# Graph stage of a two-layer graph and expert network: both matrix products as sums of half-precision products, degrees taken earlier

## The chip, the cores and the metric

The kernel runs on one core of a Trainium2 chip. What is timed is the device time in microseconds of one execution. Executions of the kernel before took 1640.42, 1648.84 and 1653.16 us; the median is 1648.84 us.

## The reference, cut to what matters

625 nodes with 768 features go through four steps, each added to its input: a normalized-adjacency graph layer, an attention and expert layer, a graph attention layer and a second expert layer. The change lies in the first of them:

```
edge_index = jnp.stack([src, dst])                 # 20625 edges, one loop per node among them
x = x + _L0_gnn_ref(_layernorm(x), edge_index, L0_gnn_W, L0_gnn_b)

def _L0_gnn_ref(x, edge_index, W, b):              # (cut)
    row, col = edge_index with one more loop per node
    deg  = segment_sum(ones, col)                  # how many edges end in a node
    dinv = rsqrt(deg)
    h    = x @ W                                   # 625x768 by 768x768
    msg  = h[row] * (dinv[row] * dinv[col])[:, None]
    return segment_sum(msg, col) + b
```

The kernel writes this with a matrix C of edge counts (625 x 625): out = dinv * ((C + I)^T (dinv * (z W))) + b, where z is the normalized x. C's zeros also give the two masks of the later graph attention layer.

## The kernel before, in words

Nodes are held as NT = 5 tiles of P = 125 rows, features as KC = 6 chunks of 128. Every engine has its own instruction stream, written out by hand in order; semaphores order the engines among each other, and a wait holds all that is behind it on its engine. There is no planner. PSUM has 8 banks of 512 float32 columns.

**Counts.** SyncE's queue starts the input transfers and then, from `raw01`, the writes of zeros to `x_slots` and `y_slots` (L825 to L831). For each of 165 chunks of 125 edges VectorE builds two one-hot blocks (`one_hot`, L1370 and L1371) and TensorE multiplies them (`edge_chunk`, L1992 and L1995). Chunks fall into six groups. After a group ScalarE and VectorE part the packed sums (`upper_counts`, `lower_counts`) and VectorE adds them to `CT` (`upper_added` L1391, `lower_added` L1401). Group 5 is the last. VectorE norms the rows into `z` on the way.

**First product.** TensorE transposes z in 30 pieces (L1976); VectorE and ScalarE copy them out of PSUM by turns (L1325, L1017). Then TensorE makes z W in float32, for each tile six chunks by 512 and by 256 columns (L2019), and ScalarE copies each tile to `xf` (L1045).

**Masks and degrees.** TensorE transposes C (L2029). VectorE makes the bfloat16 mask out of it (L1449) and sums the degrees (L1451), takes their root (`root_of`, L1303 to L1307) and scales xf (L1459). GpSimd meanwhile makes a float32 mask `absent` of CT (L936) and adds it to the logarithm of CT (L1042, L938).

**Second product.** For each tile i, TensorE makes C^T xf in float32, five tiles by 512 and by 256 columns (L2038); VectorE adds the own row (L1494), scales and adds to `xres` (L1496), takes mean and variance, norms the row into `z` (L1485) and splits its heads with ScalarE (L1055, L1057, L1488), all in `heads_normed`. Bank pairs alternate, so product i waits until VectorE has read product i - 2.

**The fence** after it (`fence(..., F_GRAPH)`) lets an engine go on once PE, VectorE, ScalarE and GpSimd have all come there. The attention of the next stage starts with TensorE's L2054.

Of the kernel before, what the change touches and what calls it, by code (L numbers as in the profile page):

```python
# [82 lines left out]
def bass_gnn_moe_stack(nc, x, src, dst, gnn_w, vecs, gate0, gate1, units0, units_s, units1,  # L83
                       bias_out, w_heads, attn_lr, out):
    ctx = ExitStack()
    with ctx:
# [1203 lines left out]
        def _(dve):  # L1290
# [30 lines left out]
            def transposed_out():  # L1321

                for c in range(0, KC, 2):
                    dve.wait_ge(s_tp, KC * (count["tp"] // 3) + c + 1)
                    nc.vector.tensor_copy(tD[:, c, :].rearrange("p (t n) -> p t n", t=NT),  # L1325
# [1092 lines left out]
```

## Time and profile before

| What | Value |
|---|---|
| Executions | 1640.42, 1648.84, 1653.16 us |
| Profiled execution, its own time | 1650.27 us |
| Its span | 1648.7 us |
| Mean granted clock of TensorE | 0.95 |
| PE busy | 1492.9 us, 91% |
| VectorE busy | 1276.5 us, 77% |
| ScalarE busy | 858.5 us, 52% |
| GpSimd busy | 331.3 us, 20% |

The profile is of one execution. PE is TensorE's matrix products, PEld its loads of the stationary operand, DVE is VectorE, ACT ScalarE, POOL GpSimd. Busy shares are means over the whole span; a stage is to be read by itself. A granted clock of 1.00 is 2.4 GHz, one of 0.50 is 1.2 GHz. A line number is that of the instruction in the kernel.

### The profile page before, as it was taken

How to read it: one execution, taken by the hardware profiler on the slowest of the kernel's cores; microseconds unless marked ns; L12 is line 12 of the kernel's file. 1: busy time of each engine (PE TensorE's matmuls, PEld its weight loads, DVE VectorE, ACT ScalarE, POOL GpSimd, SP SyncE). 2: the span in 40 equal slices, each digit the busy share in tenths (PEclk: the TensorE clock that was granted, in tenths of full speed). 3: DMA queues.
4: the chain of work that ended last, by engine and by line, in shares of the span. 5: the costliest groups of instructions: out<-in, count | busy, mean ns of one | idle time of the engine just before them, and what ended most of it. 6: DMA issues, size and time to landing. Idle time of an engine off the chain costs nothing.

```text
span 1648.7 us, 36612 instructions
## 1 busy us (share of the span) xinstructions
PE 1492.9 (91%) x14493; PEld 1271.4 (77%) x14493; DVE 1276.5 (77%) x2195; ACT 858.5 (52%) x1220; POOL 331.3 (20%) x254
## 2 busy tenths in 40 slices
PE   7987887887799999999999779966999999999996
PEld 5664545665567899999999554436899999999995
DVE  8998376775556678888888778967888878888785
ACT  1112116775544567776765234554666666666661
POOL 0004003665030000000003036755420000000050
PEclk9998898999799999999999887986999999999999
DMA  7640000000465688898886110123988888888883
GB/s 203 157 112 0 0 1 10 1 1 5 169 190 179 229 276 290 289 315 297 299 296 210 52 30 26 32 94 96 336 290 288 294 298 300 284 300 287 296 281 104
DMA packets 55554, 297.59 MB, mean 180 GB/s; under 512 B 14063, under 2 KB 14319, under 8 KB 32433
## 3 DMA queue, kind: packets, MB, share of 16 engines
q1 hardware_dynamic: 41761, 263.23, 47.0%
q0 software_dynamic: 13712, 33.26, 7.3%
q8 instruction: 53, 0.87, 0.2%
q14 instruction: 28, 0.23, 0.0%
HBM read 264.07 MB, written 32.34 MB: 180 GB/s over the span
## 4 chain that ended last, share of the span: by engine, by line
PE 58%; DVE 7%; DMA 3%; POOL 3%; ACT 2%; issue 2%; SPq 0%; DVEq 0%; ACTq 0%; POOLq 0%
PE ps L727 13%; PE ps L706 9%; PE ps L708 9%; PE ps L710 9%; PE ps L2190 5%; PE ps L2173 5%; PE ps L2302 3%; POOL wl L980 2%; DMA ext<-in_units 2%; DVE wl L583 1%; PE ps L739 1%; PE ps L690 1%; DVE big L1842 1%; DMA xf<-y_slots,slots_i 1%; PE ps L2137 1%
## 5 line engine op out<-in xcount | busy, mean ns | idle before, releaser
L706 PE MATMUL ps<-big,wh 128*128 128x176 f16 x2160 | 495.3, 239 | 8.5 <-DVE wl L583 6.6
L710 PE MATMUL ps<-big,wl 128*128 128x176 f16 x2160 | 495.4, 238 | 0.0
L708 PE MATMUL ps<-big,wh 128*128 128x176 f16 x2160 | 495.4, 238 | 0.0
L727 PE MATMUL ps<-big,wh 128*128 128x176 f16 x2160 | 262.8, 238 | 3.1 <-DVE big L617 3.1
L727 PE MATMUL ps<-big,wl 128*128 128x176 f16 x1080 | 248.9, 239 | 0.0
L583 DVE SCALAR_TENSOR_TENSOR wl<-ext,wh 128x2304 f16<-128x2304 f32 x90 | 229.6, 2551 | 0.9 <-issue 0.6
L583 DVE SCALAR_TENSOR_TENSOR wl<-raw,wh 128x2304 f16<-128x2304 f32 x90 | 229.4, 2549 | 0.0
L502 ACT ACTIVATE wh<-raw 128x2304 f16<-128x2304 f32 x90 | 190.4, 2117 | 58.2 <-PE ps L727 53.7
L706 PEld LDWEIGHTS ps<-big,wh 128*128 128x128 f16 x2160 | 208.3, 96 | 12.5 <-DVE wl L583 6.8
L502 ACT ACTIVATE wh<-ext 128x2304 f16<-128x2304 f32 x90 | 190.5, 2117 | 50.0 <-PE ps L727 34.5
L708 PEld LDWEIGHTS ps<-big,wh 128*128 128x128 f16 x2160 | 210.8, 98 | 0.2
L710 PEld LDWEIGHTS ps<-big,wl 128*128 128x128 f16 x2160 | 207.8, 96 | 0.0
L727 PEld LDWEIGHTS ps<-big,wh 128*128 128x128 f16 x2160 | 188.2, 97 | 4.7 <-DVE big L617 4.0
L1992 PE MATMUL ps<-wl 126*128 126x314 f16 x660 | 113.7, 300 | 20.9 <-DVE wl L1371 20.9
L945 POOL TENSOR_TENSOR ext<-raw,ext 125x625 f16<-125x625 f32 x60 | 80.3, 1339 | 150.4 <-ACT ext L1086 149.8
L727 PEld LDWEIGHTS ps<-big,wl 128*128 128x128 f16 x1080 | 104.4, 97 | 0.0
L980 POOL TENSOR_TENSOR wl<-wl,logs 125x625 f32<-125x625 f32 x60 | 83.2, 1413 | 67.8 <-DVE wl L1870 67.8
L469 POOL DMA_DIRECT2D y_slots<-big x16 | 11.7, 733 | 419.7 <-ACT big L532 419.7
L2302 PE MATMUL ps<-raw,wh 125*65 125x512 f32 x240 | 86.2, 507 | 6.2 <-ACT raw L1216 6.2
L1992 PEld LDWEIGHTS ps<-wl 126*128 126x128 f16 x660 | 59.6, 99 | 37.2 <-DVE wl L1371 16.4
L613 DVE TENSOR_TENSOR big<-ps,ext 128x176 f32<-128x176 f32 x108 | 36.5, 338 | 66.6 <-ACT ext L525 66.5
L463 POOL DMA_DIRECT2D big<-x_slots x17 | 12.7, 745 | 343.6 <-PE ps L690 305.1
(352 smaller groups left out, 2819.6 us busy)
## 6 DMA issues: line engine op xcount, KB each, us to landing
raw<-in_units SPq DMA_DIRECT2D x54, 1152.0 KB, 5.5
ext<-in_units SPq DMA_DIRECT2D x54, 1152.0 KB, 6.4
raw<-in_units SPq DMA_DIRECT2D x36, 1153.0 KB, 6.0
ext<-in_units SPq DMA_DIRECT2D x36, 1153.0 KB, 7.1
raw<-in_units_s SPq DMA_DIRECT2D x16, 769.0 KB, 4.5
ext<-in_units_s SPq DMA_DIRECT2D x16, 769.0 KB, 4.4
x_slots<-raw SPq DMA_DIRECT2D x1, 8976.0 KB
big<-x_slots POOLq DMA_DIRECT2D x17, 528.0 KB, 8.7
```

The costliest lines, as they stand in the source:

```text
L502: nc.scalar.activation(wh[:, u % RING, 0:ph.wide], raw[u % RING][:, 0:ph.wide], ACT.Copy, scale=WS).then_inc(ph.hi, 1)
L583: nc.vector.scalar_tensor_tensor(out=wl[:, u % RING, 0:ph.wide], in0=raw[u % RING][:, 0:ph.wide], scalar=WS, in1=wh[:, u % RING, 0:ph.wide ...
L706: nc.tensor.matmul(o, wh[:, u % RING, w_], x_, start=c == 0 and m == 0, stop=False, skip_group_check=True)
L708: nc.tensor.matmul(o, wh[:, u % RING, w_], xTl[:, c, 0:ph.n], start=False, stop=False, skip_group_check=True)
L710: ins = nc.tensor.matmul(o, wl[:, u % RING, w_], x_, start=False, stop=c == KC - 1, skip_group_check=True)
L727: ins = nc.tensor.matmul(o, l_[:, u % RING, w_], r_, start=first and k == 0 and c % 2 == 0, stop=last and k == 2, skip_group_check=True)
L945: nc.gpsimd.tensor_tensor(pT[:, 1, h % 2, :, own], key_blocks(n), pT[:, 0, h % 2, :, own], ALU.subtract).then_inc(s_wlo, 1)
L980: nc.gpsimd.tensor_tensor(power[:, (h * NT + t) % 4, :], power[:, (h * NT + t) % 4, :], logs[:, t, :], ALU.add).then_inc(s_masked, 1)
L1992: nc.tensor.matmul(ps[:, at + i * BANK:at + i * BANK + TH], hot[0:k, s, i * P:i * P + 128], hot[0:k, s, TP:TP + TH], start=first, stop=las ...
L2173: ins = nc.tensor.matmul(shared_up(j)[:, 0:n], l_[:, j % RING, w_], r_[:, c, t0 * P:t1 * P], start=c == 0 and k == 0, stop=c == KC - 1 and ...
L2190: ins = nc.tensor.matmul(shared_sum(t)[:, n0:n1], l_[:, j % 2, own], r_[:, j % RING, D + n0:D + n1], start=fresh and k == 0, stop=last and ...
L2302: ins = nc.tensor.matmul(sumsT[:, n0:n1], values[:, t, h, :], prob[:, t, n0:n1], start=t == 0, stop=t == NT - 1)
```

## The change

- **First product.** z is transposed as before, but the first three chunks already between the count products of group 5, the other three after it. ScalarE writes the float16 high parts (`xsh`, `rows_high`), VectorE the rests (`xsl`, `rows_low`). W is scaled by 64 and split too: `wgh` on ScalarE, `wgl` on VectorE, ahead of the last additions to CT. z W becomes three float16 products: high by high, rest by high, high by rest (`node_products`).
- **Degrees.** After tiles 0 and 1 of the first product, TensorE multiplies CT by a column of ones (25 products of one column). VectorE takes the root from them.
- **Rows scaled.** dinv is applied while z W leaves PSUM: `node_high` (ScalarE, float16 `hth`) and `node_low` (VectorE, rest `htl`). The scaling pass L1459 goes.
- **Counts split.** `CTh` (ScalarE) and `CTl` (VectorE) are the float16 high part and rest of CT. The second product is CTh by hth, CTh by htl, CTl by hth; the own row comes in by an identity, so the addition L1494 goes.
- **Masks.** The turns of CT go one by one behind the tiles of the first product (`counts_turned`); VectorE's loop is now: `node_low(t)`, `masked_counts(t)`, then the addition of the bias row to `xres` (before: in one go at L1443).
- **GpSimd.** `absent` lies in `z` and waits for `node_low(0)`.
- **Normed rows.** z of a tile is written by ScalarE (scale and bias from VectorE, one small operation more there), not by VectorE's L1485.

The diff, cut: lines that are only names and constants, and longer removed blocks, are left out.

```diff
...
-absent = wl[0:P, :, :].rearrange("p a n -> p (a n)").bitcast(F32)[:, 0:NT * T]\
-    .rearrange("p (t n) -> p t n", t=NT)
+absent = z[:, :, :].rearrange("p t d -> p (t d)")[:, 0:NT * T].rearrange("p (t n) -> p t n", t=NT)
+CTh = wl[0:P, :, :].rearrange("p a n -> p (a n)")[:, 2400:2400 + NT * T].rearrange("p (t n) -> p t n", t=NT)
+CTl = wl[0:P, :, :].rearrange("p a n -> p (a n)")[:, 5600:5600 + NT * T].rearrange("p (t n) -> p t n", t=NT)
+wgh = raw01[:, 0, 0:KC * D // 2].bitcast(F16).rearrange("p (c n) -> p c n", c=KC)
...
+def z0_turned(c):
+    at = (4 * BANK) + c % 3 * NT * 128
+    return ps[:, at:at + NT * 128].rearrange("p (t n) -> p t n", t=NT)[:, :, 0:P]
+def node_sum(t):
+    return bank(t % 3 * 2, 2)[0:P, 0:D]
...
-    pool.wait_ge(s_unp, 3 * len(GROUPS))
+    pool.wait_ge(s_nl, NL_H + 1)
     nc.gpsimd.tensor_scalar(absent, CT, 0.0, NEG, ALU.is_equal, ALU.mult).then_inc(s_logs, 1)
     pool.wait_ge(s_logs, 2)
     nc.gpsimd.tensor_tensor(logs[:, :, :], logs[:, :, :], absent, ALU.add).then_inc(s_logs, 1)
...
+    def rows_high(half):
+        act.wait_ge(s_tp, 3 * half + 3)
+        for c in range(3 * half, 3 * half + 3):
+            nc.scalar.activation(xsh[:, c, :].rearrange("p (t n) -> p t n", t=NT), z0_turned(c), ACT.Copy)\
+                .then_inc(s_nh, 1)
+    def node_high(t):
+        act.wait_ge(s_hmm, t + 1)
+        nc.scalar.activation(hth[:, t, :], node_sum(t), ACT.Copy, scale=rs[:, 3, t:t + 1]).then_inc(s_nh, 1)
...
-    for g in range(1, len(GROUPS)):
+    for g in range(1, len(GROUPS) - 1):
         upper_counts(g)
-    transposed_out()
+    act.wait_ge(s_zero, 48)
+    act.wait_ge(s_wg, 16)
+    for c in range(KC):
+        nc.scalar.activation(wgh[:, c, :], wg[:, c, :], ACT.Copy, scale=WS).then_inc(s_nh, 1)
+    rows_high(0)
+    upper_counts(len(GROUPS) - 1)
+    rows_high(1)
     act.wait_ge(s_unp, 3 * len(GROUPS))
+    nc.scalar.activation(CTh, CT, ACT.Copy).then_inc(s_nh, 1)
+    root()
+    count["sq"] += 1
+    act.wait_ge(s_var, count["sq"])
+    node_high(0)
+    node_high(1)
     nc.scalar.activation(logs[:, :, :], CT, ACT.Ln, bias=least[:, 0:1]).then_inc(s_logs, 1)
-    for t in range(NT):
-        act.wait_ge(s_hmm, t + 1)
-        nc.scalar.activation(xf[:, t, :], ps[0:P, (t % 2) * 1024:(t % 2) * 1024 + D], ACT.Copy)\
-            .then_inc(s_hev, 1)
-    root()
+    for t in range(2, NT):
+        node_high(t)
     act.wait_ge(s_logs, 3)
     for t in range(NT):
         count["sq"] += 1
...
+        nc.scalar.activation(z[:, t, :], xres[:, t, :], ACT.Identity, bias=pair[:, 2, t, 0:1],
+                             scale=pair[:, 3, t, 0:1])
     fence(act, F_GRAPH)
-    act.wait_ge(s_zero, 48)
...
+    def rows_low(half):
+        dve.wait_ge(s_nh, NH_Z + 3 * half + 3)
+        for c in range(3 * half, 3 * half + 3):
+            nc.vector.tensor_tensor(xsl[:, c, :].rearrange("p (t n) -> p t n", t=NT), z0_turned(c),
+                                    xsh[:, c, :].rearrange("p (t n) -> p t n", t=NT),
+                                    ALU.subtract).then_inc(s_nl, 1)
...
     g = len(GROUPS) - 1
+    rows_low(0)
     lower_counts(g)
+    rows_low(1)
+    for c in range(KC):
+        dve.wait_ge(s_nh, NH_W + c + 1)
+        nc.vector.scalar_tensor_tensor(out=wgl[:, c, :], in0=wg[:, c, :], scalar=WS, in1=wgh[:, c, :],
+                                       op0=ALU.mult, op1=ALU.subtract).then_inc(s_nl, 1)
     upper_added(g)
     lower_added(g)
-    transposed_out()
-    dve.wait_ge(s_vec[0], 16)
...
     step(nc.vector.tensor_scalar(upto[:, :, :], upto[:, :, :], 0.0, None, ALU.is_ge))
     gates_split(0)
+    dve.wait_ge(s_deg, 1)
+    nc.vector.tensor_scalar(rs[:, 0, :], bank(6)[0:P, 0:NT], 1.0, None, ALU.add).then_inc(s_var, 1)
+    dve.wait_ge(s_nh, NH_CT + 1)
+    nc.vector.tensor_tensor(CTl, CT, CTh, ALU.subtract).then_inc(s_nl, 1)
+    root_of(dinv[:, :])
+    step(nc.vector.tensor_scalar(rs[:, 3, :], dinv[:, :], 1.0 / WS, None, ALU.mult))
+    nc.vector.memset(dot[0:1, 0:1], 0.0).then_inc(s_var, 1)
+    def node_low(t):
+        dve.wait_ge(s_nh, NH_H + t + 1)
+        nc.vector.scalar_tensor_tensor(out=htl[:, t, :], in0=node_sum(t), scalar=rs[:, 3, t:t + 1],
+                                       in1=hth[:, t, :], op0=ALU.mult, op1=ALU.subtract).then_inc(s_nl, 1)
+    def masked_counts(i):
+        dve.wait_ge(s_cT, i + 1)
+        nc.vector.tensor_scalar(mask[:, i, :].rearrange("p (k n) -> p k n", k=NT), tiles5(bank(6, 2), P), 0.0,
+                                NEG, ALU.is_equal, ALU.mult).then_inc(s_cdv, 1)
+    dve.wait_ge(s_vec[0], 16)
+    dve.wait_ge(s_vec[1], 16)
     for t in range(NT):
...
+        node_low(t)
+        masked_counts(t)
+        nc.vector.tensor_tensor(xres[:, t, :], xres[:, t, :], vec[:, 0, :], ALU.add)
...
+        step(nc.vector.scalar_tensor_tensor(out=tmp[:, 0:1], in0=mv[:, t, 0:1], scalar=-1.0, in1=inv[:, 0:1],
+                                            op0=ALU.mult, op1=ALU.mult))
         nc.vector.memset(dot[0:1, 0:1], 0.0).then_inc(s_var, 1)
-        nc.vector.tensor_scalar(z[:, t, :], xres[:, t, :], mv[:, t, 0:1], inv[:, 0:1],
-                                ALU.subtract, ALU.mult)
...
     for i in range(NT):
         dve.wait_ge(s_agg, i + 1)
-        step(nc.vector.tensor_tensor(z[:, i, :], ps[0:P, (i % 2) * 1024:(i % 2) * 1024 + D], xf[:, i, :],
-                                     ALU.add))
-        nc.vector.scalar_tensor_tensor(out=xres[:, i, :], in0=z[:, i, :], scalar=dinv[:, i:i + 1],
+        nc.vector.scalar_tensor_tensor(out=xres[:, i, :], in0=bank(i % 2 * 2, 2)[0:P, 0:D], scalar=dinv[:, i:i + 1],
                                        in1=xres[:, i, :], op0=ALU.mult, op1=ALU.add).then_inc(s_aggv, 1)
         dve.wait_ge(s_aggv, i + 1)
         heads_normed(i)
...
+    def rows_transposed_0(half):
+        for c in range(3 * half, 3 * half + 3):
             for t in range(NT):
-                ins = nc.tensor.transpose(o[:, t * 128:t * 128 + P], rows_[:, t, c * 128:(c + 1) * 128],
-                                          ident[0:P, 0:P])
+                ins = nc.tensor.transpose(z0_turned(c)[:, t, :], z[:, t, c * 128:(c + 1) * 128], ident[0:P, 0:P])
             ins.then_inc(s_tp, 1)
-            count["tp"] += 1
-    def transposed(k):
-        pe.wait_ge(s_tpe, 3 * k)
-        pe.wait_ge(s_tpa, 3 * k)
     def edge_chunk(c, g, first, last):
...
             pe.wait_ge(s_unp, 3 * g - 5)
         for c in range(j0 * EU, j1 * EU):
             edge_chunk(c, g, c == j0 * EU, c == j1 * EU - 1)
-    pe.wait_ge(s_rowsok, R_Z0)
-    pe.wait_ge(s_unp, 3 * len(GROUPS) - 5)
-    transpose_rows(z)
-    transposed(1)
-    pe.wait_ge(s_wg, 16)
+            if g == len(GROUPS) - 1 and c == (j0 + 3) * EU - 1:
+                pe.wait_ge(s_rowsok, 1)
+                pe.wait_ge(s_unp, 3 * len(GROUPS) - 5)
+                rows_transposed_0(0)
+    def node_products(t, n0, n1):
+        for k, (l_, r_) in enumerate(((xsh, wgh), (xsl, wgh), (xsh, wgl))):
+            if t == 0 and n0 == 0 and k == 0:
+                pe.wait_ge(s_nh, NH_Z + KC)
+                pe.wait_ge(s_nh, NH_W + KC)
+            if t == 0 and n0 == 0 and k == 1:
+                pe.wait_ge(s_nl, NL_Z + KC)
+            for c in range(KC):
+                if t == 0 and n0 == 0 and k == 2:
+                    pe.wait_ge(s_nl, NL_W + c + 1)
+                ins = nc.tensor.matmul(node_sum(t)[:, n0:n1], l_[:, c, t * P:(t + 1) * P], r_[:, c, n0:n1],
+                                       start=k == 0 and c == 0, stop=k == 2 and c == KC - 1)
+        if n1 == D:
+            ins.then_inc(s_hmm, 1)
+    def counts_turned(i):
+        if i:
+            pe.wait_ge(s_cdv, i)
+        for k in range(NT):
+            ins = nc.tensor.transpose(bank(6, 2)[0:P, k * 128:k * 128 + P], CT[:, k, i * P:(i + 1) * P],
+                                      ident[0:P, 0:P])
+        ins.then_inc(s_cT, 1)
+    pe.wait_ge(s_nl, NL_Z + 3)
+    rows_transposed_0(1)
     pe.wait_ge(s_unp, 3 * len(GROUPS) - 2)
...
+    for t in range(2):
+        node_products(t, 0, BANK)
+        node_products(t, BANK, D)
     pe.wait_ge(s_unp, 3 * len(GROUPS))
     for i in range(NT):
-        if i >= 2:
-            pe.wait_ge(s_cdv, i - 1)
-        o = bank(4 + 2 * (i % 2), 2)
         for k in range(NT):
-            ins = nc.tensor.transpose(o[0:P, k * 128:k * 128 + P], CT[:, k, i * P:(i + 1) * P],
-                                      ident[0:P, 0:P])
-        ins.then_inc(s_cT, 1)
-    pe.wait_ge(s_rowsok, R_HS)
+            ins = nc.tensor.matmul(bank(6)[0:P, i:i + 1], CT[:, k, i * P:(i + 1) * P], ones[0:P, 0:1],
+                                   start=k == 0, stop=k == NT - 1)
+    ins.then_inc(s_deg, 1)
+    pe.wait_ge(s_var, 2)
+    counts_turned(0)
+    for t in range(2, NT):
+        if t == 3:
+            pe.wait_ge(s_nl, NL_H + 1)
+        if t == 4:
+            pe.wait_ge(s_nl, NL_H + 2)
+        node_products(t, 0, BANK)
+        if t == 4:
+            counts_turned(3)
+        node_products(t, BANK, D)
+        counts_turned(t - 1 if t < 4 else 4)
+    pe.wait_ge(s_nl, NL_CT + 1)
+    pe.wait_ge(s_nl, NL_H + NT)
     for i in range(NT):
         if i >= 2:
             pe.wait_ge(s_aggv, i - 1)
         for n0, n1 in ((0, BANK), (BANK, D)):
+            o = bank(i % 2 * 2, 2)[0:P, n0:n1]
+            for r_ in (hth, htl):
+                for k in range(NT):
+                    nc.tensor.matmul(o, CTh[:, k, i * P:(i + 1) * P], r_[:, k, n0:n1],
+                                     start=r_ is hth and k == 0, stop=False)
+                nc.tensor.matmul(o, ident16[0:P, 0:P], r_[:, i, n0:n1], start=False, stop=False)
             for k in range(NT):
-                ins = nc.tensor.matmul(ps[0:P, (i % 2) * 1024 + n0:(i % 2) * 1024 + n1],
-                                       CT[:, k, i * P:(i + 1) * P], xf[:, k, n0:n1],
-                                       start=k == 0, stop=k == NT - 1)
+                ins = nc.tensor.matmul(o, CTl[:, k, i * P:(i + 1) * P], hth[:, k, n0:n1], start=False,
+                                       stop=k == NT - 1)
         ins.then_inc(s_agg, 1)
     fence(pe, F_GRAPH)
```

## Rows read from the trace of the kernel before

**Rows 1.** Page, part 2: GB/s in 40 slices of 41.2 us.
```profile
GB/s 203 157 112 0 0 1 10 1 1 5 169 190 179 229 276 290 289 315 297 299 296 210 52 30 26 32 94 96 336 290 288 294 298 300 284 300 287 296 281 104
```

**Rows 2.** Timeline, PE: start, length, engine, line, out<-in, count [idle before <-releaser].
```profile
137.38 1.23 PE L1976 MATMUL ps<-ident,z 125*128 125x125 f32 x10
...
152.22 40.59 PE L2019 MATMUL ps<-ext,big 128*125 128x512 f32 x120 [0.83 <-issue]
...
205.28 34.92 PE L2038 MATMUL ps<-xf,big 125*125 125x512 f32 x100 [5.97 <-DVE dot L1463]
252.62 0.60 PE L2054 MATMUL ps<-ident,wh 125*128 125x125 f16 x4 [12.41 <-DVEq L405]
```

**Rows 3.** Timeline, DVE, from the last counts to the masks.
```profile
140.70 1.47 DVE L1378 SCALAR_TENSOR_TENSOR wl<-wh,ps 125x1256 f32<-125x1256 f32 x1 [4.48 <-ACT wh L1032]
...
144.28 1.79 DVE L1401 SCALAR_TENSOR_TENSOR big<-wl,big 125x1565 f32<-125x1565 f32 x1
...
151.11 5.95 DVE L1435 CAST ident<-ident 128x128 f16<-128x128 f32 x1
...
164.63 4.43 DVE L1443 TENSOR_TENSOR xres<-xres,vec 125x768 f32<-125x768 f32 x5
193.47 0.81 DVE L1449 TENSOR_SCALAR mask<-ps 125x625 bf16<-125x625 f32 x1 [24.41 <-PE ps L2029]
```

**Rows 4.** Timeline, POOL, same stretch.
```profile
146.16 10.81 POOL L936 TENSOR_SCALAR wl<-big 125x3125 f32<-125x3125 f32 x1 [140.34 <-DVE big L1401]
157.06 6.80 POOL L938 TENSOR_TENSOR logs<-logs,wl 125x3125 f32<-125x3125 f32 x1
```

**Rows 5.** Timeline, DVE: first tile, then the fourth, of the second product.
```profile
214.52 0.96 DVE L1494 TENSOR_TENSOR z<-ps,xf 125x768 f32<-125x768 f32 x1 [9.29 <-PE ps L2038]
...
237.26 0.95 DVE L1494 TENSOR_TENSOR z<-ps,xf 125x768 f32<-125x768 f32 x1
238.25 1.02 DVE L1496 SCALAR_TENSOR_TENSOR xres<-z,dinv,xres 125x768 f32<-125x768 f32 x1
...
242.64 0.15 DVE L1483 TENSOR_SCALAR pair<-pair 125x1 f32<-125x1 f32 x1
242.84 0.68 DVE L1485 TENSOR_SCALAR z<-xres,mv,pair 125x768 f32<-125x768 f32 x1
...
244.84 0.95 DVE L1494 TENSOR_TENSOR z<-ps,xf 125x768 f32<-125x768 f32 x1
```

**Rows 6.** Timeline, ACT: heads of the fourth tile and of the last.
```profile
242.94 0.94 ACT L1055 ACTIVATE wh<-ext,pair 125x768 f16<-125x768 f32 x1 [1.89 <-DVE dot L1484]
...
251.36 0.92 ACT L1057 ACTIVATE wl<-ext,pair 125x768 f16<-125x768 f32 x1
```

**Rows 7.** Timeline, PE: float16 products of a later stage.
```profile
562.48 0.59 PE L2190 MATMUL ps<-wh,big 128*125 128x512 f16 x2
...
563.13 0.38 PE L2190 MATMUL ps<-wh,big 128*125 128x256 f16 x2
...
563.46 0.38 PE L2190 MATMUL ps<-wh,big 128*125 128x256 f16 x2
```

**Rows 8.** Timeline, PE: ten float32 products of 64 columns.
```profile
281.54 1.30 PE L2110 MATMUL ps<-both,big 128*125 128x64 f32 x10 [0.58 <-ACT big L1093]
```

**Rows 9.** Windows: busy PE, PEld, DVE, ACT, POOL, granted clock, DMA share, GB/s.
```profile
147.00:152.00 5.00, 4.39 (x20) 3.74 (x20) 2.42 (x3) 1.26 (x2) 5.00 (x1) 0.50 0.00 0
205.20:210.00 4.80, 4.71 (x6) 2.11 (x7) 0.03 (x1) 0.00 (x0) 0.00 (x0) 0.50 0.00 0
```

**Rows 10.** One line each: DVE beside GpSimd; duration ns min/median/max, first and last start.
```profile
L1853 DVE SCALAR_TENSOR_TENSOR cols<-cols x12: 166/606/1428, 955.0 to 1068.5; 125x5 f32<-125x5 f32 x12
L1870 DVE SCALAR_TENSOR_TENSOR wl<-ps,branch,ext x60: 851/858/872, 968.9 to 1093.1; 125x625 f32<-125x625 f32 x60
```

**Rows 11.** Timeline at 990 us: DVE's longest L1853.
```profile
989.90 1.43 DVE L1853 SCALAR_TENSOR_TENSOR cols<-cols 125x5 f32<-125x5 f32 x1
```

**Rows 12.** Timeline at 990 us, POOL.
```profile
989.80 1.50 POOL L980 TENSOR_TENSOR wl<-wl,logs 125x625 f32<-125x625 f32 x1
```

More of the change, by code:

```diff
@@ L43 @@
 BANK = 512
+NH_W, NH_Z, NH_CT, NH_H = 0, KC, 2 * KC, 2 * KC + 1
+NL_Z, NL_W, NL_CT, NL_H = 0, KC, 2 * KC, 2 * KC + 1
 C_ZERO, C_ALL = 2, 14
 F_GRAPH, F_MHA = range(1, 3)
-R_Z0, R_HS = range(1, 3)
 def f16_pair(v):
@@ L391, in bass_gnn_moe_stack @@
         s_done = sem("s_done")
-        s_tpa = sem("s_tpa")
         ph_0 = Phase(sem, "layer0", I0 // 128, True, 2 * NS)
@@ L1319, in squares_asked @@
                 nc.vector.tensor_scalar(rs[:, 2, :], rs[:, 3, :], 1.0, None, ALU.mult).then_inc(s_var, 1)
[L1321 to L1325, printed above, removed]
-                                          tiles5(bank(4, 2), 128)).then_inc(s_tpe, 1)
-                    count["tp"] += 1
+            def rows_low(half):
[4 more added lines that the diff above has]
+                                            ALU.subtract).then_inc(s_nl, 1)
             def gates_split(layer):
@@ L1441, in _ @@
             gates_split(0)
-            for t in range(NT):
-                ins = nc.vector.tensor_tensor(xres[:, t, :], xres[:, t, :], vec[:, 0, :], ALU.add)
-            step(ins)
-            for i in range(NT):
-                dve.wait_ge(s_cT, i + 1)
-                counts = tiles5(bank(4 + 2 * (i % 2), 2), P)
-                nc.vector.tensor_scalar(mask[:, i, :].rearrange("p (k n) -> p k n", k=NT), counts, 0.0, NEG,
-                                        ALU.is_equal, ALU.mult)
-                ins = nc.vector.tensor_reduce(rs[:, 0, i:i + 1], counts, AX.XY, ALU.add)
-                ins.then_inc(s_cdv, 1)
@@ L1453, in _ @@
-            dve.wait_ge(s_cdv, NT)
-            nc.vector.tensor_scalar(rs[:, 0, :], rs[:, 0, :], 1.0, None, ALU.add).then_inc(s_var, 1)
-            root_of(dinv[:, :])
-            dve.wait_ge(s_hev, NT)
-            for t in range(NT):
-                ins = nc.vector.tensor_scalar(xf[:, t, :], xf[:, t, :], dinv[:, t:t + 1], None, ALU.mult)
-            count["v"] += 1
-            ins.then_inc(s_v, 1)
-            dve.wait_ge(s_v, count["v"])
-            nc.vector.memset(dot[0:1, 0:1], 0.0).then_inc(s_rowsok, 1)
@@ L2006, in _ @@
                     edge_chunk(c, g, c == j0 * EU, c == j1 * EU - 1)
-            pe.wait_ge(s_rowsok, R_Z0)
-            pe.wait_ge(s_unp, 3 * len(GROUPS) - 5)
-            transpose_rows(z)
-            transposed(1)
-            pe.wait_ge(s_wg, 16)
-            pe.wait_ge(s_unp, 3 * len(GROUPS) - 2)
-            for t in range(NT):
-                if t >= 2:
-                    pe.wait_ge(s_hev, t - 1)
-                for n0, n1 in ((0, BANK), (BANK, D)):
-                    for c in range(KC):
-                        ins = nc.tensor.matmul(ps[0:P, (t % 2) * 1024 + n0:(t % 2) * 1024 + n1],
-                                               tD[:, c, t * P:(t + 1) * P], wg[:, c, n0:n1],
-                                               start=c == 0, stop=c == KC - 1)
-                ins.then_inc(s_hmm, 1)
+                    if g == len(GROUPS) - 1 and c == (j0 + 3) * EU - 1:
+                        pe.wait_ge(s_rowsok, 1)
+                        pe.wait_ge(s_unp, 3 * len(GROUPS) - 5)
+                        rows_transposed_0(0)
```

24 lines of the change are left out of this document (6 added, 18 removed).

## The prediction, made before the change was run

> **What bounds the kernel now.** The page's busy shares say that TensorE is the bound, 91% of the span. That is a mean; the change touches only the graph stage, so I read that stage in timelines, engine by engine. The stage runs from the end of the count products at 137.4 us to the attention's first turn at 252.6 [rows 2]. The reader is to see a relay, not one busy engine. First TensorE: 40.6 us of float32 product, 152.2 to 192.8 [rows 2], VectorE idle for 24.4 us of it [rows 3]. Then VectorE: mask, degrees and scaling, TensorE idle 6.0 us [rows 2]. Then TensorE's first tile of the second product, 9.2 us to the first row of [rows 5]. From there VectorE sets the end: a tile every 7.58 us (237.26 to 244.84 [rows 5]), while TensorE is done at 240.2 and waits 12.4 us at the fence [rows 2]. So four things count: when C is complete, when the scaled rows are complete, how long the first tile takes, and VectorE's chain per tile.
>
> **Prices.** Three float16 products of 512 columns take 0.65 us and three of 256 take 0.33 [rows 7]: 0.217 and 0.11 each. A tile of the first product is 18 of each, 5.9 us (float32: 40.6 / 5 = 8.1, with a slow start); of the second 17 of each (5 + 1 + 5 + 1 + 5), 5.6 us. Five turns cost 0.6 (ten in 1.23 [rows 2]), with arrival 0.7. VectorE: 125x768 with two inputs 1.0 us, small steps 0.2 (242.64 to 242.84) [rows 5]; 625 columns from PSUM 0.8, 1565 with two inputs 1.8 [rows 3]. ScalarE: 768 columns 0.9 [rows 6].
>
> **At no cost.** The first 15 turns (1.9 us) stand among count products that wait for VectorE; the six `wgh` copies (5.4 us by rows 6) and three high parts (2.4) lie on ScalarE between two groups. If that cover fails, the count stage grows by up to 1.9. ScalarE's wait for the zero writes moves ahead of them; SyncE issues nothing new, and the traffic is over by the end of the third slice, 123.7 us [rows 1]. Were it late, everything behind it, group 5's parting too, would wait. `CTh` (3125 columns, some 3.7 us) runs while TensorE is at tile 1, the logarithm beside tiles 2 and 3.
>
> **Up to the first product.** VectorE ends `lower_counts` of group 5 near 142.5 (140.7 + 1.5 and the tail [rows 3]). New behind it: three rests of z, 2.2 us, begun at 142.7 when ScalarE has the high parts: 144.9. Then six `wgl`, pitch 0.93, 5.6 us: 150.5. The two additions to CT, 3.6 us, now end at 154.1 instead of 146.0. TensorE's first half tile follows `wgl` piece by piece: 150.9. Its engine is mostly idle from 138 on, and 147 to 152 us now shows granted clock 0.50, 1.2 GHz, after such a pause [rows 9]; so I charge tile 0's second half double, 4.0: 154.9. Tile 1: 160.8.
>
> **Degrees.** 25 float32 products of one column do not occur in the trace. Below: 0.12, a turn with the same stationary size [rows 2]; above: 0.24, the same at 1.2 GHz. The nearest, 64 columns, shows ten in 1.30 [rows 8]; I take 0.13, 3.3 us: 164.1. VectorE then adds one (0.2), makes `CTl` (3125 columns, 3.6), takes root and scale (seven small steps, 1.4): 169.3. `node_high(0)` 0.9, `node_low(0)` 1.0: 171.3, released on TensorE tile 2 long before.
>
> **GpSimd becomes a gate.** Its `absent` (10.8 us) and addition to the logarithms (6.8) [rows 4] now begin at 171.3, beside VectorE's new loop. What happens then is in the trace twice. VectorE's copy of the identity (128 columns) took 5.95 us, from 151.1 to 157.06; GpSimd's first operation ended at 156.97 [rows 3, 4]. And L1853, five elements with both inputs in SBUF, takes 0.166 us at best, 1.43 at worst [rows 10]; that one ended at 991.33, with GpSimd's operation, 989.80 to 991.30 [rows 11, 12]. L1870, with one input in PSUM, stays within 851 to 872 ns in the same stage, GpSimd busy or not [rows 10]. `node_low` and `masked_counts` read PSUM and at most one SBUF tensor: free. The addition of the bias row, `xres` + `vec`, has two SBUF inputs: it is held. So tile 0's addition waits until 171.3 + 10.8 = 182.1 and ends at 183.1; GpSimd's second operation, behind it, until 189.9; tile 1's addition until then, 190.9. Behind each addition stand the next rest and mask, and behind the mask TensorE's next turn. `node_low(2)` and mask 2: 192.7. Turn 3, 0.7: 193.4; tile 4's last part, 2.0: 195.4; its high part and rest, 1.9: 197.3. TensorE's tiles 2, 3 and the first part of 4 (16 us) end before, even with one stretch at 1.2 GHz.
>
> The Trainium skill (SBUF — State Buffer, section Who interferes with whom) says the same: a VectorE instruction with two SBUF inputs contends with a GpSimd instruction that reads SBUF, and whoever is second blocks fully. By that rule the sum is the one here; by counting busy times alone it would be the first rival's. The rows agree.
>
> **Second product.** First tile 5.6: 203.0 (float32 took 9.2, 205.3 to 214.5 [rows 2, 5]). VectorE's pitch per tile: 7.58 less the own row's addition 0.99 (237.26 to 238.25) plus one small step 0.20: 6.79. L1485, 0.68, is worth nothing: ScalarE starts its head copy at 242.94 and VectorE can't go on before 243.9 [rows 5, 6]. Four tiles 27.2, the last 7.8 - 0.8 = 7.0 up to the fence: 237.2. TensorE's 5.6 per tile is under 6.79, so it doesn't bind. ScalarE has `z` of the last tile behind L1057, which ends at 252.28 now; 0.9 more passes the fence by 0.6 [rows 6]: 237.8.
>
> **The sum.** 252.6 - 237.8 = 14.8 us. The profiled execution took 1650.27, so 1635.5; it stood 1.4 over the median 1648.84. I say **1635**. Parts: the rows are scaled at 197.3 instead of 205.3 (8.0), the first tile 3.6, the chains 5 x 0.79 = 3.9, ScalarE's end -0.6. Bounds: tile 0 at full clock -2; degrees at 0.24 each +3; the first tile of the second product partly at 1.2 GHz, as 205 to 210 now [rows 9], +2.8. That gives 1633 to 1642, before the scatter of executions.
>
> **Rivals.**
> - *Nothing is held* (12%). If VectorE's additions slip past GpSimd, TensorE leads: turn 0 at 165.0, tile 2 170.9, turn 1 after mask 0 172.8, tile 3 178.7, turn 2 179.4, tile 4 with turn 3 186.0, rests 187.9, 9.4 earlier. Time 1626. Against it: rows 10 to 12.
> - *Held twice as long* (11%). If GpSimd's second operation starts before the waiting addition, tile 0's addition ends at 189.9, mask 1 at 191.7, turn 2 at 192.4, all of tile 4 behind it: 200.9, with its first part at 1.2 GHz 204.8. Time 1639 to 1643. Against: the identity's copy came through before GpSimd's second operation at 157.06 [rows 3, 4], not after it.
> - *The clock stays at 1.2 GHz* (4%), the case that ends slower. Price in the second product: 11.1 us per tile instead of 5.6, above VectorE's 6.79; five are 55.6 + 7.0 + 0.6 = 63.2 against 5.6 + 27.2 + 7.0 + 0.6 = 40.4, so +22.8: 1658; with tile 1 (+5.9) and the degrees (+2.7) slow as well, 1667. It decides from four slow tiles on (+17.2). For it: pauses up to 6 us before dense work, twice in the new order. Against: now the slow stretch after a pause of 6.0 us holds from 205.3 to about 210 only, and the other four tiles average 6.4 us, the full rate [rows 2, 5, 9].
> - *The forecast* has 73%.
>
> **Numbers.** From no change, this kernel's measurement tells about 1%, 16.5 us, so 1632.4; its three executions lie 12.7 apart. My forecast is 0.9% down, hence mostly within: of its 73% I give 29 to faster and 43 to the same, 1 to slower. With the rivals: faster 0.41, same 0.54, slower 0.05. The range runs from the first rival with scatter, 1623, to the second with scatter, 1646.
>
> **What would show it.** Second product from 197 us (187 or 201 to 205 by the rivals); two additions of `xres` of about 11 and 6 us instead of 1, ending with GpSimd's operations; TensorE idle some 5 us before turn 2; degrees 3.3 us; tile 0 of the second product under 6 us; tile pitch 6.8; VectorE waiting about 1.1 for ScalarE's heads where L1485 stood; the attention's first turn at 238. The forecast falls if the additions take 1 us each, if the pitch stays at 7.6, or if the count products end later than 137.4.

## The result, and the profile after

| | before | after |
|---|---|---|
| Median, us | 1645.49 (1640.42 to 1653.16, 4 runs) | 1627.47 (1624.75 to 1631.32, 4 runs) |
| Ratio, 95% interval | | 0.9888 [0.984, 0.9936] |
| Span of the profiled execution | 1648.7 | 1623.2 |
| Attention's first turn, end of the stage | 252.6 | 237.4 |

A later comparison of the same two kernels, with 6 and 11 runs, gave 0.9887 [0.9853, 0.9921], 1628.41 against 1647.14. The change makes the kernel faster by 1.1%, some 18 us, of which the stage shows 15.2. The engines' totals tell almost nothing of it (part 1 of the page of the kernel after: busy us, share of the span, instructions; before, PE had 1492.9 and 91%):

```profile
PE 1474.0 (91%) x14673; PEld 1270.6 (78%) x14673; DVE 1275.0 (79%) x2196; ACT 873.8 (54%) x1235; POOL 331.8 (20%) x254
```

The stage is to be read engine by engine, as before. TensorE's timeline of the kernel after; columns as in [rows 2]:

```profile
127.59 1.76 PE L2001 MATMUL ps<-ident,z 125*128 125x125 f32 x15
...
149.21 8.24 PE L2041 MATMUL ps<-raw,big 128*125 128x512 f16 x55 [0.44 <-DVE raw L1463]
157.29 7.23 PE L2064 MATMUL ps<-ones,big 125*125 125x1 f32 x50
164.85 1.41 PE L2051 MATMUL ps<-ident,big 125*125 125x125 f32 x5 [0.33 <-DVE rs L1475]
166.06 8.49 PE L2041 MATMUL ps<-raw,big 128*125 128x512 f16 x36
...
174.93 6.01 PE L2041 MATMUL ps<-raw,big 128*125 128x512 f16 x36
182.07 0.81 PE L2051 MATMUL ps<-ident,big 125*125 125x125 f32 x5 [1.13 <-DVE mask L1491]
...
187.15 2.13 PE L2041 MATMUL ps<-raw,big 128*125 128x256 f16 x18
192.05 1.41 PE L2051 MATMUL ps<-ident,big 125*125 125x125 f32 x5 [2.77 <-DVE mask L1491]
193.94 2.36 PE L2088 MATMUL ps<-xf,wl 125*125 125x512 f16 x5 [0.47 <-DVE xf L1485]
...
237.42 0.60 PE L2107 MATMUL ps<-ident,wh 125*128 125x125 f16 x4 [13.49 <-ACTq L422]
```

Read against [rows 2], the second product starts at 193.9 instead of 205.3 and the fence opens at 237.4 instead of 252.6. But the degrees, `L2064`, take 7.2 us, and the tile behind them 8.5 where the next one takes 6.0. VectorE's timeline of the kernel after, which answers to [rows 3] and [rows 5]:

```profile
164.63 0.17 DVE L1475 TENSOR_SCALAR rs<-ps 125x5 f32<-125x5 f32 x1 [10.85 <-PE ps L2064]
164.71 3.41 DVE L1477 TENSOR_TENSOR wl<-big,wl 125x3125 f16<-125x3125 f32 x1
...
170.42 1.02 DVE L1485 SCALAR_TENSOR_TENSOR xf<-ps,rs,xf 125x768 f16<-125x768 f32 x1 [1.09 <-ACT xf L1040]
171.36 0.80 DVE L1491 TENSOR_SCALAR mask<-ps 125x625 bf16<-125x625 f32 x1
172.07 8.30 DVE L1499 TENSOR_TENSOR xres<-xres,vec 125x768 f32<-125x768 f32 x1
...
181.94 0.94 DVE L1499 TENSOR_TENSOR xres<-xres,vec 125x768 f32<-125x768 f32 x1
...
184.45 5.91 DVE L1499 TENSOR_TENSOR xres<-xres,vec 125x768 f32<-125x768 f32 x1
190.28 1.00 DVE L1485 SCALAR_TENSOR_TENSOR xf<-ps,rs,xf 125x768 f16<-125x768 f32 x1
...
192.79 1.01 DVE L1485 SCALAR_TENSOR_TENSOR xf<-ps,rs,xf 125x768 f16<-125x768 f32 x1
...
201.87 1.02 DVE L1529 SCALAR_TENSOR_TENSOR xres<-ps,dinv,xres 125x768 f32<-125x768 f32 x1 [6.50 <-PE ps L2092]
...
206.04 0.17 DVE L1513 RECIPROCAL pair<-pair 125x2 f32<-125x2 f32 x1 [0.69 <-ACT pair L1081]
...
209.44 1.01 DVE L1529 SCALAR_TENSOR_TENSOR xres<-ps,dinv,xres 125x768 f32<-125x768 f32 x1
...
216.22 1.01 DVE L1529 SCALAR_TENSOR_TENSOR xres<-ps,dinv,xres 125x768 f32<-125x768 f32 x1
...
229.79 1.01 DVE L1529 SCALAR_TENSOR_TENSOR xres<-ps,dinv,xres 125x768 f32<-125x768 f32 x1
```

Two of the five additions of the bias row take 8.3 and 5.9 us instead of 0.94, and they stand beside these two of GpSimd (its timeline, same kernel; [rows 4] is before):

```profile
171.54 10.82 POOL L953 TENSOR_SCALAR z<-big 125x3125 f32<-125x3125 f32 x1 [165.71 <-DVE xf L1485]
182.44 7.11 POOL L955 TENSOR_TENSOR logs<-logs,z 125x3125 f32<-125x3125 f32 x1
```

The tiles of the second product follow each other by 6.78 us (209.44 to 216.22) instead of 7.58. TensorE's clock, in windows of the kernel after (columns as in [rows 9]: busy PE, PEld, DVE, ACT, POOL, granted clock):

```profile
157.00:165.00 8.00, 7.67 (x56) 7.59 (x53) 0.37 (x2) 0.17 (x1) 0.00 (x0) 0.74 0.01 2
165.00:170.00 5.00, 5.00 (x15) 3.23 (x16) 4.11 (x8) 0.67 (x2) 0.00 (x0) 0.50 0.00 0
...
194.00:199.00 5.00, 5.00 (x14) 2.75 (x15) 1.37 (x2) 0.00 (x0) 0.00 (x0) 0.56 0.00 0
```

So there are two stretches near 1.2 GHz: during and behind the one-column products, and at the start of the second product.

**Outside the stage.** The two profiled spans differ by 25.5 us, the stage by 15.2. The other 10.3 come later, where the change touches nothing: 2.9 have gathered when the head products of the graph attention layer start (18.1 us earlier than before), and 7.3 lie between the first and the last of these. The head products, one line each, of the kernel before, of the kernel after, and of the kernel before once more (count, duration ns min/median/max, first and last start):

```profile
L2302 PE MATMUL ps<-raw,wh x240: 257/492/1117, 972.3 to 1102.6; 125*65 125x512 f32 x60, 125*65 125x113 f32 x60
```
```profile
L2355 PE MATMUL ps<-raw,wh x240: 257/492/1117, 954.2 to 1077.2; 125*65 125x512 f32 x60, 125*65 125x113 f32 x60
```
```profile
L2302 PE MATMUL ps<-raw,wh x240: 257/492/1117, 976.5 to 1098.5; 125*65 125x512 f32 x60, 125*65 125x113 f32 x60
```

That stretch took 130.3 us in the first profile of before, 123.0 after, and 122.0 in the second profile of before: the kernel before has both values. In the kernel after once more it took 123.7, and in eight variants of it 121.9 to 128.4. It is the spread of single executions, not the change.

### The profile page after: what moved, and what is told of

Its sections match the earlier page's. It is cut to its first block, busy times and chain, and to the rows that moved or that the text cites. A ratio compares the mean times of both kernels' runs of the same rounds, so it can differ in the third digit from the quotient of the medians.

```text
span 1623.2 us, 36989 instructions
## 1 busy us (share of the span) xinstructions
PE 1474.0 (91%) x14673; PEld 1270.6 (78%) x14673; DVE 1275.0 (79%) x2196; ACT 873.8 (54%) x1235; POOL 331.8 (20%) x254
## 4 chain that ended last, share of the span: by engine, by line
PE 59%; DVE 7%; POOL 3%; ACT 2%; issue 2%; DMA 2%; SPq 0%; DVEq 0%; ACTq 0%
PE ps L744 14%; PE ps L723 9%; PE ps L725 9%; PE ps L727 9%; PE ps L2243 5%; PE ps L2226 5%; POOL wl L997 2%; PE ps L2355 2%; DMA ext<-in_units 2%; PE ps L756 1%; DVE wl L600 1%; PE ps L707 1%; DVE big L1875 1%; PE ps L2327 1%; PE ps L2297 1%
## 5 line engine op out<-in xcount | busy, mean ns | idle before, releaser
L2355 PE MATMUL ps<-raw,wh 125*65 125x512 f32 x240 | 80.7, 481 | 5.7 <-ACT raw L1245 5.6
```

What stands on the lines that cost most here:

```text
L2355: ins = nc.tensor.matmul(sumsT[:, n0:n1], values[:, t, h, :], prob[:, t, n0:n1], start=t == 0, stop=t == NT - 1)
```

## The experiments

"First turn" is the start of the attention's first product, where the stage ends: 252.5 and 252.6 in two profiles of before, 237.4 and 236.8 in two of after. It is a far sharper measure than a kernel's time: of unchanged kernels it repeats within 0.1 us before and 0.6 after, and the 0.6 lies in the first tile of the second product (7.93 and 7.33 us).

**again_before.** No edit.

> The kernel before once more, unchanged. The changed kernel's profile is 25.5 us shorter, but only 15.2 of it lie in the graph stage (attention's first turn at 252.6 before, at 237.4 after); 10.3 more lie in the graph attention layer's head products, whose first and last start lay 130.3 us apart before and 123.0 after, and in the gathers before them. Theory: that part is the executions' own spread. Then this trace has the attention's first turn at 252.6 within 0.3, but the head products spread over another length than 130.3, somewhere in 121 to 132. Rival: the change shortened it. Then 130 again.

Measured: 1644.66 us beside 1653.03 on the same chip; first turn 252.5; head products 122.0 us. The stage repeats within 0.1 us, and the 130.3 us of the later layer belonged to that one execution.

**x_add.** All five additions of the bias row before the degrees, away from GpSimd.

```diff
+            dve.wait_ge(s_vec[0], 16)
+            for t in range(NT):
+                nc.vector.tensor_tensor(xres[:, t, :], xres[:, t, :], vec[:, 0, :], ALU.add)
             dve.wait_ge(s_deg, 1)
...
                 masked_counts(t)
-                nc.vector.tensor_tensor(xres[:, t, :], xres[:, t, :], vec[:, 0, :], ALU.add)
```

> The changed kernel with the five additions of the bias row to xres moved to VectorE's wait before the degrees (153.8 to 164.6 us), away from GpSimd's operations. Theory (the held additions set when the rows are complete): TensorE then leads; the second product starts at 190 instead of 193.9, the attention's first turn comes at 231 to 234 instead of 237.4, and each addition takes 0.9 us. Rival 1 (they were held but hid behind TensorE): 237.4. Rival 2, the size of my prediction (9.4 us): 228.

Timelines of `x_add`, VectorE and TensorE, and a window:

```profile
154.12 4.43 DVE L1476 TENSOR_TENSOR xres<-xres,vec 125x768 f32<-125x768 f32 x5
...
194.37 1.02 DVE L1530 SCALAR_TENSOR_TENSOR xres<-ps,dinv,xres 125x768 f32<-125x768 f32 x1 [5.18 <-PE ps L2093]
```
```profile
188.62 1.26 PE L2089 MATMUL ps<-xf,wl 125*125 125x512 f16 x5 [1.59 <-DVE xf L1488]
```
```profile
189.00:194.00 5.00, 5.00 (x33) 3.74 (x31) 0.19 (x1) 0.00 (x0) 0.11 (x1) 1.00 0.00 0
```

First turn 229.9, so 7.5 us earlier. Two parts: the second product starts 5.3 earlier (188.62 against 193.94), since neither VectorE's rests nor TensorE's turns wait behind a held addition; and its first tile takes 5.75 instead of 7.93, at clock 1.00 instead of 0.56. Before it TensorE now has one pause of 1.59 us, where it had two, of 2.77 and 0.47. The other traces go the same way: `x_first32`, `x_best` and `x_bestz`, with the 1.59 us alone, have 5.74 to 5.75 us, and the kernels with 2.0 or 2.8 us and then 1.1 have 7.3 to 8.6. That the pauses lower the clock is read from this pattern; no run changed them alone. The hold is real and costs 7.5 us, the clock's part included. My range, 231 to 234, left out that part, and was missed.

**x_z.** The normed rows back on VectorE.

```diff
-                nc.scalar.activation(z[:, t, :], xres[:, t, :], ACT.Identity, bias=pair[:, 2, t, 0:1],
-                                     scale=pair[:, 3, t, 0:1])
...
-                step(nc.vector.scalar_tensor_tensor(out=tmp[:, 0:1], in0=mv[:, t, 0:1], scalar=-1.0, in1=inv[:, 0:1],
-                                                    op0=ALU.mult, op1=ALU.mult))
+                nc.vector.tensor_scalar(z[:, t, :], xres[:, t, :], mv[:, t, 0:1], inv[:, 0:1],
+                                        ALU.subtract, ALU.mult)
```

> The changed kernel with the normed rows back on VectorE and the small operation for ScalarE's bias gone. Theory (VectorE waits for ScalarE's head copies anyway; the row operation is hidden, the small step is not): VectorE's pitch per tile 6.58 instead of 6.78, ScalarE no longer past the fence, the attention's first turn at 235.6 instead of 237.4. Rival (moving the rows to ScalarE shortened the chain): pitch 7.3 or more, first turn at 240 or later.

First turn 235.3, 2.1 earlier; the tile pitch is 6.60 (208.72 to 215.32) instead of 6.78. So this part of the change costs time: VectorE waits for ScalarE's heads in either order, and ScalarE's `z` of the last tile passes the fence. Of the 2.1, 0.5 came from a somewhat shorter first tile (7.44 us), which is within what the kernel after shows without any edit; 1.6 are the edit's.

**x_ctl.** `CTl` made before the wait for the degrees.

```diff
+            dve.wait_ge(s_nh, NH_CT + 1)
+            nc.vector.tensor_tensor(CTl, CT, CTh, ALU.subtract).then_inc(s_nl, 1)
             dve.wait_ge(s_deg, 1)
             nc.vector.tensor_scalar(rs[:, 0, :], bank(6)[0:P, 0:NT], 1.0, None, ALU.add).then_inc(s_var, 1)
-            dve.wait_ge(s_nh, NH_CT + 1)
-            nc.vector.tensor_tensor(CTl, CT, CTh, ALU.subtract).then_inc(s_nl, 1)
```

> The changed kernel with CTl made before VectorE waits for the degrees instead of after them. Theory (its 3.4 us stand on the path degrees, root, rows, GpSimd, additions): node_low(0) ends near 168 instead of 171.4, the attention's first turn comes at 234 to 235. Rival (TensorE's tiles 2 and 3 lead from there): the first turn stays at 237.4 within 0.5.

First turn 235.0, 2.4 earlier. The first rest, `node_low(0)`, starts at 167.35 instead of 170.42, the second product at 190.87 instead of 193.94: 3.1 in both, and 0.6 given back in a slower first tile.

**x_deg.** The degrees from the float16 counts, which needs a float16 column of ones and a wait for `CTh`. The degrees then come from the high part alone; up to 2048 edges between two nodes it holds the count exactly.

```diff
+            pe.wait_ge(s_nh, NH_CT + 1)
...
-                    ins = nc.tensor.matmul(bank(6)[0:P, i:i + 1], CT[:, k, i * P:(i + 1) * P], ones[0:P, 0:1],
+                    ins = nc.tensor.matmul(bank(6)[0:P, i:i + 1], CTh[:, k, i * P:(i + 1) * P], ones16[0:P, 0:1],
```

> The changed kernel with the degrees from the float16 high part of the counts (CTh by a float16 column of ones) instead of float32. Theory (a float32 product is two instructions in the trace, 50 for 25 products, 7.2 us): float16 takes 2 to 2.5 us, everything behind moves 4.5 to 5.2 earlier, first turn of the attention at 232.2 to 233. Rival (a product of one column costs its stationary operand's load, 0.29 us whatever the type): 7.2 us again, 237.4.

TensorE's timeline of `x_deg`:

```profile
158.02 1.56 PE L2067 MATMUL ps<-ones,wl 125*125 125x1 f16 x25
...
160.55 6.02 PE L2043 MATMUL ps<-raw,big 128*125 128x512 f16 x36
```

25 records instead of 50, 1.56 us instead of 7.23, and the tile behind them 6.02 instead of 8.49: the granted clock is 1.00 from 157 to 170. First turn 232.0, 5.4 earlier. TensorE ends that tile 8.0 earlier (166.57 against 174.55), but VectorE's chain (`CTl`, root, rests, held additions) passes on only 4.9 (`node_low(0)` at 165.48); the first tile gives the rest.

**x_first32.** The first product in float32 again, with everything else as after: no rests, no split of W.

```diff
-                for k, (l_, r_) in enumerate(((xsh, wgh), (xsl, wgh), (xsh, wgl))):
+                for k, (l_, r_) in enumerate(((tD, wg),)):
...
-                nc.vector.scalar_tensor_tensor(out=wgl[:, c, :], in0=wg[:, c, :], scalar=WS, in1=wgh[:, c, :],
-                                               op0=ALU.mult, op1=ALU.subtract).then_inc(s_nl, 1)
+                dve.sem_inc(s_nl, 1)
```

> The changed kernel with the first product back in float32 (the splits of z and W left out of it, ScalarE copies the turned z in float32). Theory (what the float16 pairs win on TensorE, 1.8 us per tile, is given back by the eleven splitting operations on VectorE before the counts are complete, so tiles 0 and 1 end at about the same time, and only tiles 2 to 4 are later): the counts are complete at 145.5 instead of 152.7, the attention's first turn comes at 239 to 242 instead of 237.4. Rival (the pairs made the first product's gain): 246 or later.

TensorE's timeline of `x_first32`:

```profile
142.53 18.70 PE L2039 MATMUL ps<-ext,big 128*125 128x512 f32 x48 [3.46 <-DVE wl L1406]
161.07 6.33 PE L2062 MATMUL ps<-ones,big 125*125 125x1 f32 x50
...
197.83 1.26 PE L2086 MATMUL ps<-xf,wl 125*125 125x512 f16 x5 [1.59 <-DVE xf L1482]
```

First turn 239.1: the pairs of the first product are worth 1.7 us, not the ten that 40.6 us of float32 against five tiles of 6.0 suggest. Float32 tiles 0 and 1 need no `wgl` and end at 161.1, only 3.8 later; behind them VectorE's chain is the same one. The start is 3.9 later, and the first tile at full clock (5.74) gives 2.2 back, so without the clock's part the pairs are worth 3.9.

**x_second32.** The second product in float32, so without `htl`, `CTh` and `CTl`; the own row still by the identity.

```diff
-                    for r_ in (hth, htl):
-                        for k in range(NT):
-                            nc.tensor.matmul(o, CTh[:, k, i * P:(i + 1) * P], r_[:, k, n0:n1],
-                                             start=r_ is hth and k == 0, stop=False)
-                        nc.tensor.matmul(o, ident16[0:P, 0:P], r_[:, i, n0:n1], start=False, stop=False)
+                    nc.tensor.matmul(o, ident[0:P, 0:P], xf[:, i, n0:n1], start=True, stop=False)
                     for k in range(NT):
-                        ins = nc.tensor.matmul(o, CTl[:, k, i * P:(i + 1) * P], hth[:, k, n0:n1], start=False,
+                        ins = nc.tensor.matmul(o, CT[:, k, i * P:(i + 1) * P], xf[:, k, n0:n1], start=False,
```

> The changed kernel with the second product in float32, the own row by a float32 identity (CTh, CTl, and the rests of the scaled rows left out). Theory (VectorE's chain of 6.8 us per tile covers 5.5 us of float16; float32 with six products takes about 7.7 and becomes the bound, but 3.4 us of CTl and 1.0 of each rest go from VectorE): the attention's first turn within 2 us of 237.4. Rival (the pairs are what shortened this part): 245 or later.

TensorE's timeline of `x_second32`, the first groups of tiles 0, 2 and 3 (tiles are counted from 0):

```profile
188.16 1.09 PE L2085 MATMUL ps<-xf,ident 125*125 125x512 f32 x2 [0.43 <-DVEq L1485]
...
203.71 1.02 PE L2085 MATMUL ps<-xf,ident 125*125 125x512 f32 x2
...
211.45 1.02 PE L2085 MATMUL ps<-xf,ident 125*125 125x512 f32 x2
```

First turn 234.8, which is 2.6 earlier than with the pairs; I had expected it within 2 of 237.4 and missed. TensorE is the slower one now (pitch 7.74 against 6.78). From the first tile's row on VectorE to the last one's that makes 31.0 us instead of 27.9, 3.0 more, since the kernel after needs 7.57 for its first pitch. But the product starts 5.8 earlier, for `CTl` and the five rests are gone from VectorE's chain. In this kernel, as its parts are placed, the second product's pairs cost more on VectorE than they save on TensorE. Most of that is a matter of place: with the pairs kept, moving `CTl` alone brings 2.4 (`x_ctl`).

**again_after, x_best, x_bestz.** Five rounds on one chip. `x_best` joins `x_deg` and `x_ctl`, with two additions before the degrees, where VectorE is idle, and three behind the loop; `x_bestz` is that and `x_z`.

```diff
+            for t in range(2):
+                nc.vector.tensor_tensor(xres[:, t, :], xres[:, t, :], vec[:, 0, :], ALU.add)
...
                 masked_counts(t)
+            for t in range(2, NT):
                 nc.vector.tensor_tensor(xres[:, t, :], xres[:, t, :], vec[:, 0, :], ALU.add)
```

> The changed kernel once more, unchanged, timed in five rounds. Theory (the change is worth what the stage shows, 252.6 - 237.4 = 15.2 us; the 10.3 us beyond it in the first comparison of profiles were the executions' own): a ratio of 0.9905 to 0.991, the attention's first turn at 237.4 again, the head products over another length than 123.0 us. Rival (something after the stage is shorter too): 0.985 or less.

> The changed kernel with three edits together: degrees from CTh in float16, CTl and two additions of the bias row in VectorE's wait before the degrees, the other three additions behind the loop, when GpSimd is done. Theory (with the degrees at 1.6 us, nothing held and the clock at 2.4 GHz throughout, TensorE leads from tile 0 to the second product): second product starts at 182, its first tile takes 5.8, the attention's first turn comes at 223 to 224.5; a ratio to the kernel before of 0.982 to 0.983. Rival (the edits win the same microseconds, so that together they bring no more than the best alone): 229 or later, ratio 0.986.

> The kernel of the three edits, with the normed rows on VectorE as well. Theory: pitch per tile 6.58 instead of 6.78 and no row operation of ScalarE past the fence, so 2.0 us less: the attention's first turn at 221 to 222.5, ratio 0.981 to 0.982; the gain over the kernel of three edits is too small for the timed ratio and shows in the trace alone. Rival (TensorE's second product becomes the bound before that): the same as the kernel of three edits.

| | median us | ratio to before | first turn |
|---|---|---|---|
| again_after | 1628.41 | 0.9887 [0.9853, 0.9921] | 236.8 |
| x_best | 1619.03 | 0.9832 [0.9802, 0.9863] | 223.6 |
| x_bestz | 1616.31 | 0.9813 [0.9784, 0.9842] | 222.3 |

`x_bestz`, TensorE's and VectorE's timelines and a window:

```profile
158.68 1.56 PE L2068 MATMUL ps<-ones,wl 125*125 125x1 f16 x25
...
182.63 1.26 PE L2092 MATMUL ps<-xf,wl 125*125 125x512 f16 x5 [1.59 <-DVE xf L1488]
```
```profile
174.14 0.81 DVE L1494 TENSOR_SCALAR mask<-ps 125x625 bf16<-125x625 f32 x1 [4.34 <-PE ps L2054]
...
183.12 2.69 DVE L1502 TENSOR_TENSOR xres<-xres,vec 125x768 f32<-125x768 f32 x3
```
```profile
165.00:170.00 5.00, 5.00 (x36) 4.10 (x35) 2.56 (x3) 3.74 (x3) 5.00 (x1) 1.00 0.00 0
```

Now VectorE waits for TensorE's turns (4.34 us before the third mask), with GpSimd at work beside it, and TensorE runs at full clock. The kernel after itself came out a little better than I had expected of it (0.9887, said 0.9905 to 0.991; first turn 236.8, said 237.4), and its head products took 123.7 us, hardly the other length that I had named. Both versions beat both kernels: `x_bestz` by 30.8 us against before, of which the stage shows 30.3 (252.6 - 222.3). Between the two the first turn shows `x_bestz` 1.3 ahead, where I had said 2.0; their times can't be told apart.

## Why the prediction held, step by step

The time came out 7.5 us under my 1635, inside the range. At 1.1% it lies just beyond the 1% within which I had put the larger chance (0.54, faster 0.41); the interval takes in both sides. Most of that is the base: I took 14.8 off the profiled 1650.27, while the median of before, now with more runs, is 1645.49: 4.8 us. The stage gave 15.2 instead of 14.8, and 2.3 are left for the spread of executions. By the time alone the first rival, with 1626 us, was nearer than I; only the rows decide against it. That the stage came so close is in part luck, for misses of 2 to 4 us in both directions cancelled; these are the terms of the sum:

- **Up to tile 1: the path right, 3.5 us too late.** Cover for the turns held (`L2001` lies among the count products; those end at 136.8, said 137.4). Tile 1 ended at 157.3, not 160.8: the clock was not slow in tile 0 (1.00 from 137 to 157), for which I had charged 2.0, and the splits of W ended at 149.2, not 150.5. That clock is not there in every execution: in the kernel after once more it was 0.86 from 137 to 149, and tile 1 ended at 158.4.
- **Degrees: mis-sized, 3.3 us said, 7.2 measured.** I priced 25 products by "ten in 1.30", but a float32 product has two records each, so those ten records are five products [rows 8], and 25 products are 50 records, of 0.145 us each. My upper bound, 0.24 each, 6 us, was below the truth, too; it was the fallen clock that passed it, for in `x_z`, with a mean clock of 0.93 from 157 to 165, they took 5.72 us. Here the clock fell with them (0.74 on the mean of 157 to 165, then 0.50), which stretched tile 2 to 8.5. Both errors, tile 1 early and degrees long, cancelled: degrees done at 164.6, said 164.1, and the first rest ended at 171.4, said 171.3. It was not one execution's chance: in six profiles (the kernel after twice, and four variants) whose tile 1 ended between 157.3 and 158.8 the float32 degrees all ended between 164.5 and 164.6. What fixes that end no run shows. `x_deg` shows the price: 5.4 us.
- **GpSimd as a gate: the mechanism right, its size too large.** I said additions of about 11 and 6 us on tiles 0 and 1. They took 8.3 on tile 0 and 5.9 on tile 2; tile 1's, at 181.94, slipped in just before GpSimd's second operation, recorded from 182.44. Second product at 193.9, said 197.3. The last steps of the path were others, too: I had TensorE's turn 3 and the last part of tile 4 wait behind the hold, but that tile was done at 189.3, and VectorE alone set the start, with the last two rests behind the held addition (ended 190.4; rest 4 from 192.79 to 193.80). And the identity's copy, which I had put first as evidence, has one SBUF input: it shows a hold, not my rule of two inputs, which rests on L1853 and now on the 8.3 and 5.9 us. The rival "nothing is held" (187.9, 1626 us) and the one held twice as long (201 to 205) are refuted by the rows; `x_add`, where nothing is held, starts at 188.6; that rival had 187.9. The Trainium skill (SBUF — State Buffer, section Who interferes with whom) has the later of the two instructions blocked fully; the 8.3 and 5.9 us agree in kind, though the first hold ended before GpSimd's record does (last section), and the rests and masks, which read PSUM, stay at 1.0 and 0.8.
- **First tile: 5.6 said, 7.9 measured.** The bound named for it, +2.8 for a start near 1.2 GHz, is what happened. I took the lower value, though the row of before [rows 9] spoke for the higher one: TensorE had just been waiting, in either kernel. I should have priced it as I priced tile 0.
- **The root's table: missed, 0.8.** VectorE's first tile has 7.57 us, not 6.78, because it waits 0.69 for `L1081`. ScalarE's timeline of the kernel after shows why:

```profile
204.51 1.28 ACT L1081 ACT_TABLE_LOAD   x1 [14.29 <-DVE pair L1507]
205.81 0.20 ACT L1081 ACTIVATE pair<-pair 125x2 f32<-125x2 f32 x1
```

The logarithm now runs behind the first root, so the root's table is loaded once more, on the path. Before, that load lay at 193.68, in ScalarE's idle time.
- **Pitch 6.79 said, 6.78 measured; moving L1485 worth nothing, and the end of ScalarE costing time: right.** Undone in `x_z`, the part brings 1.6 us without the first tile's 0.5; both of its terms, 0.6 at the fence and a small step of 0.20 per tile, stood in my sum. (`x_bestz` against `x_best`, whose first tiles are alike, has 1.6, too, counted from the start of the second product.)
- **The clock stays low: refuted.** It was 0.96 in 198 to 203, and in `x_add` 1.00 throughout the second product's first tile. Two slow stretches there were all the same.

Summed: start 3.4 earlier than said, first tile 2.3 and table 0.8 later, which leaves the first turn at 237.4, where I said 237.8.

Where did the gain come from? The rows of before and after divide the 15.2 us. The first product ends 3.5 earlier (189.3 against 192.8). From there to the second product's start it takes 4.7 us instead of 12.5, 7.8 less, for masks, degrees and scaling now run beside the first product or between its tiles. The first tile is 1.3 shorter (7.9 against 9.2). From its row on VectorE to the fifth tile's it takes 27.9 us instead of 30.3 (214.52 to 244.84 before, 201.87 to 229.79 after), 2.4 less, for the own row's addition is gone, less the root's table. The end gives 0.2.

So most of it comes from what moved, and less from half precision than the name of the change suggests. The single experiments say the same of this kernel: the pairs of the first product give 1.7 (3.9 without the clock's part), those of the second cost 2.6, and the rows on ScalarE cost 1.6. Such values hold for this kernel and must not be added up: each depends on which engine leads, and here VectorE's held additions cover much of what TensorE saves. In `x_best`, where TensorE leads up to the second product, the pairs should be worth more; by 7.9 us for a float32 tile in `x_first32` and 6.0 for one of pairs, I estimate 5.7 us for tiles 2 to 4 alone. That was not run, and neither was the scaling, the turns or the own row undone by itself. The three misplacements that the experiments mended (held additions, float32 degrees, `CTl` on the path) were worth 7.5, 5.4 and 2.4 us singly and 13.2 together (`x_best` against the kernel after of the same rounds).

## What to carry to other kernels

In a relay of engines, price a rewrite by which engine's chain sets the next start, not by the busy time that it saves: some 10 us of TensorE time were worth 1.7 to 3.9 here, and moving five additions of 0.94 us each out of GpSimd's way, two of which had been held, was worth 7.5. A value found by undoing one part holds only as long as the same engine leads. Before you price an operation by a group of records, work out from the code how many products stand behind them. And take the forecast off the median, with the profiled execution only for the terms.
